# Scores of two head halves side by side on two row halves of TensorE, with product parts and loads put in a new order, in a gated cross-attention and feed-forward layer

## What is computed

```python
x = x + tanh(g_xattn[0]) * attention(layernorm(x), ctx, ctx, Wq, Wk, Wv, Wfc, bfc)
x = x + tanh(g_ffn[0]) * ffn(layernorm(x), router_weight, sh_*, r_*)

# attention: 32 heads of 16, 8 groups of keys and values (4 heads share one)
qh = (q @ Wq.T).reshape(N, S, HEADS, HEAD_DIM).transpose(0, 2, 1, 3)
kh = (k @ Wk.T).reshape(N, S, GROUPS, HEAD_DIM).transpose(0, 2, 1, 3)   # vh alike
score = jnp.einsum('bhqd,bhkd->bhqk', qh, kh) / math.sqrt(HEAD_DIM)
out = jnp.einsum('bhqk,bhkd->bhqd', jax.nn.softmax(score, axis=-1), vh)
return out.transpose(0, 2, 1, 3).reshape(N, S, EMBED) @ Wfc.T + bfc
```

## Time and profile before

| | before |
|---|---|
| median of three runs | 955.55 us (951.3 to 956.73) |
| the profiled execution | 942.72 us |
| its span, first to last instruction | 940.9 us |
| TensorE matmuls busy | 899.5 us (96%) |
| VectorE busy | 646.6 us (69%) |
| GpSimd busy | 486.7 us (52%) |
| ScalarE busy | 343.4 us (37%) |
| mean granted TensorE clock | 0.987 |

### The profile page before, as it was taken

One profiled execution on the slowest core, in us unless ns is written; L12 is line 12 of the kernel. 1 busy time (PEld: TensorE's weight loads), 2 busy tenths in 40 slices (PEclk: granted clock), 3 DMA queues, 4 the chain that ended last, 5 costly groups with the idle time before them and its releaser, 6 DMA issues.

```text
span 940.9 us, 14873 instructions
## 1 busy us (share of the span) xinstructions
PE 899.5 (96%) x4896; PEld 697.8 (74%) x4896; DVE 646.6 (69%) x1083; ACT 343.4 (37%) x637; POOL 486.7 (52%) x485
## 2 busy tenths in 40 slices
PE   4689999999999999999999999999999999999998
PEld 3556766676677665688888888887688888888887
DVE  6678888778878887566656566567766656566566
ACT  5165566556655686212212122136212211122112
POOL 4201201300130299878766696663778766696650
PEclk9789999999999999999999999999999999999999
DMA  8863344435343420211111121111312111121102
GB/s 277 201 144 80 78 116 74 108 80 118 62 96 83 87 37 25 90 45 67 45 60 52 45 67 45 45 57 56 112 45 68 45 54 57 45 67 45 45 1 89
DMA packets 42346, 70.83 MB, mean 75 GB/s; under 512 B 5312, under 2 KB 21184, under 8 KB 42048
## 3 DMA queue, kind: packets, MB, share of 16 engines
q1 hardware_dynamic: 42304, 70.29, 27.9%
HBM read 55.33 MB, written 14.68 MB: 74 GB/s over the span
## 4 chain that ended last, share of the span: by engine, by line
PE 72%; issue 17%; DVE 4%; DMA 3%; POOL 2%; ACT 2%; SPq 0%; POOLq 0%; DVEq 0%; ACTq 0%
PE bank L1241 21%; PE bank L1243 20%; PE bank L1242 20%; PE bank L1316 3%; PE bank L1296 3%; PE bank L1306 3%; PE bank L1246 1%; POOL xa L461 1%; DMA q_scr<-qx_l 1%; POOL cx_l L430 1%; DVE mcol L887 1%; PE bank L1565 1%; DVE x_l L1206 1%; DMA wfc_raw<-wfc 1%; DMA xa<-x 1%
## 5 line engine op out<-in xcount | busy, mean ns | idle before, releaser
L887 DVE TENSOR_REDUCE mcol<-bank 128x2 f32<-128x512 f32 x256 | 169.8, 677 | 48.9 <-PE bank L1296 48.1
L1241 PE MATMUL bank<-x_l,w_h 128*128 128x512 f32 x504 | 197.5, 392 | 2.7 <-DVE u L1077 2.5
L1243 PE MATMUL bank<-x_h,w_h 128*128 128x512 f32 x504 | 196.4, 390 | 0.0
L1242 PE MATMUL bank<-x_h,w_l 128*128 128x512 f32 x504 | 196.4, 390 | 0.0
L740 ACT ACTIVATE probs<-bank 128x512 f32<-128x512 f32 x256 | 150.1, 594 | 120.6 <-PE bank L1306 119.5
L595 ACT ACTIVATE hT_h<-bank 128x512 fp32r<-128x512 f32 x72 | 43.2, 599 | 360.3 <-DVE bank L1179 351.5
L551 POOL TENSOR_TENSOR w_l<-raw,w_h 128x512 fp32r<-128x512 f32 (+1 forms) x144 | 162.1, 1159 | 2.9
L1089 DVE SCALAR_TENSOR_TENSOR xa<-bank,tgf,xa 128x512 f32<-128x512 f32 x128 | 96.1, 751 | 77.7 <-PE bank L1243 77.6
L1296 PE MATMUL bank<-k_st,q_st 65*128 65x256 f32 x512 | 114.0, 312 | 11.8 <-DMA q_st<-q_scr 7.1
L1296 PEld LDWEIGHTS bank<-k_st,q_st 65*128 65x128 f32 x512 | 92.9, 201 | 43.1 <-DVE mcol L887 16.6
L430 POOL TENSOR_TENSOR cx_l<-cx_raw,cx_h 128x512 fp32r<-128x512 f32 x12 | 15.5, 1295 | 191.4 <-ACT cx_h L595 191.4
(11 more groups left out here) (148 smaller groups left out, 1362.8 us busy)
## 6 DMA issues: line engine op xcount, KB each, us to landing
raw<-w_gu SPq DMA_DIRECT2D x36, 512.0 KB, 3.3
q_st<-q_scr SPq DMA_DIRECT2D x96, 128.0 KB, 3.8
dnraw<-w_dn SPq DMA_DIRECT2D x36, 256.0 KB, 2.6
xa<-x SPq DMA_DIRECT2D x4, 1024.0 KB, 7.6
cx_raw<-ctxT SPq DMA_DIRECT2D x16, 256.0 KB, 3.4
q_scr<-qx_h SPq DMA_DIRECT2D x16, 256.0 KB, 2.1
q_scr<-qx_l SPq DMA_DIRECT2D x16, 256.0 KB, 2.2
out<-xa SPq DMA_DIRECT2D x16, 256.0 KB, 2.0
```

What stands on the lines that cost most here:

```text
L887: v.tensor_reduce(mcol[:, par, at:at + 2], bank[u % sm_banks(n)][:, :].rearrange("p (r k) -> p r k", r=2), AX.X, ALU.max).then_inc(max_ok, 1)
L1241: mm(out, a_h, b_l, start=start, stop=False, skip_group_check=onto)
L1242: mm(out, a_l, b_h, start=False, stop=False, skip_group_check=onto)
L1243: return mm(out, a_h, b_h, start=False, stop=stop, skip_group_check=onto)
```

## The change

Heads of a chunk are dealt to two halves of the array's rows: four heads at rows 0 to 63, four at rows 64 to 127. q is stored with half the columns (`QUADS`), its weights are put in another order on the host, and k is read twice, once for each row half. The zero rows and their memset go: `SM` is 48, `MROW` 48, `ST` 49. Units on TensorE become four pairs `v` a step. A pair starts when both maxima (or both exponentials) of the last pair are done. Each half has a bank and semaphores of its own. `read_q` and `read_k` issue six transfers in place of three. `put_max` writes one row in each half.

Parts of products stand behind every pair, up to three at a time, and also cross from one step to the next. Transposes of x use one bank, output parts the other. `aT` has two copies. In SyncE's list writes of q go ahead of the reads, context loads and the write of k ahead of `put_max`. The wait ahead of `read_q` is now for the values' products of step n - 1. `m_copy` follows the fourth exponential instead of the third. `w_h0` and `w_l0` have memory of their own.

```diff
-CONSTS = 2
-SM = P // 2 + 1
+CONSTS = 1
+SM = 3 * DH
 MROW = SM
 ST = MROW + 1
+ROWS = P // 2
+QUADS = HC // 2
...
-        q_st = sb("q_st", [P, CHUNKS, HC, S], f32r, att)
+        q_st = sb("q_st", [P, CHUNKS, QUADS, S], f32r, att)
...
-        aT = sb("aT", [P, S], f32, att)
+        aT = sb("aT", [P, 2, S], f32, att)
...
+            return bank[j] if isinstance(tb, int) and tb == 0 else PJ[0]
+
+        def q_bank(tb, oc):
+
+            return PJ[(oc + 1) % 2] if isinstance(tb, int) and tb == 0 else PJ[1 if oc == 0 else 0]
+
+        def f_bank(t, bb, qt):
+
+            return PJ[qt] if isinstance(t, int) and t == BLOCKS - 1 and bb == 1 else PJ[1]
...
+            def scored(n):
+
+                sp.wait_ge(pv_ok, 4 * n)
...
                 if not fresh:
-                    sp.wait_ge(st_full, UNITS * n)
+                    scored(n)
                 sp.wait_ge(q_wr[c], 32 * (tb + 1))
-                for row, part in ((0, 0), (DH, 0), (2 * DH, 1)):
-                    src = q_scr[part, tb, c, :, bb * S:(bb + 1) * S].rearrange("(h d) q -> d h q", d=DH)
-                    sp.dma_start(r(q_st[row:row + DH, c, :, :]), src).then_inc(q_rd[c], 16)
+                for e in range(2):
+                    for row, part in ((0, 0), (DH, 0), (2 * DH, 1)):
+                        src = q_scr[part, tb, c, e * ROWS:(e + 1) * ROWS,
+                                    bb * S:(bb + 1) * S].rearrange("(h d) q -> d h q", d=DH)
+                        at = e * ROWS + row
+                        sp.dma_start(r(q_st[at:at + DH, c, :, :]), src).then_inc(q_rd[c], 16)
...
+                for e in range(2):
+                    for row, part in ((0, 0), (DH, 1), (2 * DH, 0)):
+                        src = k_scr[part, tb, :, bb * S:(bb + 1) * S].rearrange("(g d) s -> d g s", d=DH)
+                        at = e * ROWS + row
+                        sp.dma_start(r(k_st[at:at + DH, bb, :, :]), src).then_inc(k_rd[bb], 16)
...
                 for s in range(STEPS):
                     n = STEPS * t + s
-                    if s + 3 < STEPS or not last and s != 6:
+                    if s == 0 and not first:
+                        write_q_high(t, 3)
+                        write_q_low(t, 3)
+                    if not last and s >= 5:
+                        write_q_high(t + 1, s - 5)
+                        write_q_low(t + 1, s - 5)
+                    if s + 3 < STEPS or not last:
                         e = s + 3
                         tb = t if e < STEPS else t + 1
                         read_q(tb, e % STEPS // CHUNKS, e % CHUNKS, n, first and s == 0)
...
+                    if s in (0, 2) and not last:
+                        load_cx(t + 1, s)
+                        load_cx(t + 1, s + 1)
+                    if s == 4 and not last:
+                        write_k(t + 1)
                     if not last or s + 1 < STEPS:
                         put_max(n + 1, (s + 1) % CHUNKS)
...
-            g.memset(q_st[0:SM, :, :, :].bitcast(f32), 0.0).then_inc(consts, 1)
...
-                        if u == 2 and (not last or s + 1 < STEPS):
+                        if u == 3 and (not last or s + 1 < STEPS):
                             m_copy(n + 1)
...
+            def sm_pair(n, v, bb, c):
+
+                qt, g2 = v % 2, v // 2
                 banks = sm_banks(n)
-                if not (isinstance(n, int) and n == 0 and u < banks):
-                    pe.wait_ge(max_ok, UNITS * n + u + 1 - banks)
+                if not (isinstance(n, int) and n == 0 and 2 * v < banks):
+                    pe.wait_ge(max_ok, UNITS * n + 2 * v + 2 - banks)
                 for j in range(2):
...
+                    for e in range(2):
+                        rows = slice(e * ROWS, e * ROWS + SM)
+                        last = mm(bank[(2 * v + e) % banks][:, j * S:(j + 1) * S],
+                                  q_st[rows, c, 2 * g2 + j, qt * P:(qt + 1) * P],
+                                  k_st[rows, bb, 2 * c + g2, :], start=True, stop=True)
+                        if j == 1:
+                            last.then_inc(sm_full[e], 1)
+
+            def st_pair(n, v, bb, c):
+
+                kt, g2 = v % 2, v // 2
+                if not (isinstance(n, int) and n == 0 and v == 0):
+                    pe.wait_ge(exp_ok, UNITS * n + 2 * v)
+                for e in range(2):
+                    rows = slice(e * ROWS, e * ROWS + ST)
+                    mm(STB[e][:, :], k_st[rows, bb, 2 * c + g2, kt * P:(kt + 1) * P],
+                       q_st[rows, c, 2 * g2:2 * g2 + 2, :], start=True, stop=True).then_inc(st_full[e], 1)
```

In the last block the output parts of its first tile stand in steps 4 and 5, of its second in step 6, of the last batch in step 7. VectorE's list in the new order:

```diff
+                        if not last and s == 1 and u == 0:
+                            x_low(nx, 1)
+                        if not last and s == 2 and u == 0:
+                            x_low(nx, 3)
+                        if s == 7 and u == 0:
+                            a_low(n - 3, 0, last)
+                        if s == 7 and u == 2:
+                            a_low(n - 2, 1, last)
...
+                        if s == 1 and u == 3 and not first:
+                            f_sum(t - 1, 1, 0)
+                        if s == 2 and u == 1 and not first:
+                            f_sum(t - 1, 1, 1)
...
+                        if s == 6 and u == 1:
+                            f_sum(t, 0, 0)
+                        if s == 7 and u == 1:
+                            f_sum(t, 0, 1)
...
+                        if s == 4 and u == 1:
                             k_low(nx)
-                        if s in (6, 7) and u == 5:
+                        if s == 4 and u == 7:
+                            q_low(nx, 0)
+                        if s == 5 and u == 5:
+                            q_low(nx, 1)
+                        if s in (6, 7) and u == 7:
                             q_low(nx, s - 4)
```

433 lines of the change are left out of this document (213 added, 220 removed).

## The result

The changed kernel is slightly slower. Its median is 961.01 us (952.57 to 963.86, 15 runs) against 952.3 us for the kernel before on the same chip (945.75 to 961.83, 15 runs). The ratio is 1.0083, with a 95% interval of 1.0054 to 1.0112. The prediction was 932.5 us with a range of 911 to 957: wrong in sign, and the time lies outside the range. The profiled execution took 956.5 us with a span of 954.7, where before it took 942.72 and 940.9.

What follows compares the result with a forecast made beforehand. TensorE was taken to bound the middle attention blocks, VectorE less than a fifth behind. Savings of 17.7, 8 and 2 us less 4.7 lost at the start gave 23 us off 955.55, so 932.5 us, range 911 to 957.

Steps and rivals of the forecast that it cites:

- part 5: Loads: running blocks have queue room; before the first step, extra reads of q and k lose 4.7 us, bounds 2 and 8.
- The other moves: Context loads ahead of the maxima's row, x_job in one bank, second aT: free, within 1 us a block either way.
- part 2: Shape changes around each pair on TensorE: 0.19 us for entry and exit, 6.1 us a block; bounds 0 and 0.5 a pair.
- part 1: Score products of both head halves run at once on TensorE: 15.1 us less a block, bounds 0 and 15.1.
- third rival: Row halves run one after the other on TensorE, so pairs save nothing: 15 us slower, 970 us; chance 0.13.
- part 3: Pairs instead of units in the middle blocks: 77 us a block against 86.6 and 85.1, 17.7 us saved.
- the floor of 1.85: Least time of a slot, a pair and what stands behind it: scores, two maxima, release and second half's start, 1.85 us.
- part 4: First and last attention blocks: 8 us saved of 85.9 in the first, 2 us of 70.3 in the last.
- The second: Rival: the row of maxima becomes the last wait, middle blocks 81 us, last 76, kernel 953, no difference; chance 0.13.
- The first: Rival: VectorE and ScalarE hide more than granted, middle blocks 70 to 72 us, 41 us off, 914; chance 0.22.
- halves together: Sign of being right: in a middle block, a pair's two maximum products start within 0.1 us of one another.
- a gap of over 0.3 us without a semaphore: Sign of being wrong: such a gap between a product part and a pair would show the price of shape changes.

Runs made afterwards that it cites:

- the run with fillers: Changed kernel with k read for the first half only, plus unread matmuls at step 2 of every block but the first and three last-block slots: 937.85 us.

## Why the prediction was wrong

**The DMA engines (part 5) are the step that decided the sign.** It said that "In a running block the queue has room", and counted only what the reads of q cost the queue, 2.7 us of 9; the six reads of k are not in that sum. Never counted was how long the 16 engines need: 768 KB of k at some 125 GB/s is 6 us, and the reads of q follow them. The write of q's first chunk, moved behind k's reads and just ahead of its use, is not named there; it falls under "The other moves", which went down as "free, within 1 us a block either way". Against the run with k read once, k's second three reads cost 3.2 us in the third block, 5.9 in the second, and 18.6 up to the attention's end, with the clock's falls behind the waits in it. Over the three traces of that code the two blocks' costs are 3.2 to 5.6 and 2.0 to 5.9. k's doubled bytes do stand in part 5, but only for the start. Bytes and lost slack act together: with k read once the same order costs the third block's step 5 nothing (9.63 us), moving k's reads behind the write didn't help, and with the same bytes one step earlier half or more of the third block's loss went.

**The changes of shape (part 2) were mis-sized by half.** I read the 0.085 ahead of a values block and the 0.105 behind it in rows 4 as an entry and an exit. They are the ends of two changes, each of which costs both: 0.19 us a change, 0.38 a pair, 12.2 us a block instead of 6.1. The bounds (0 to 0.5) held the value; the one taken was wrong. The Trainium skill's "TensorEngine Tiling (Array Packing)", section Tiling Modes, says that a change of mode drains the engine; the trace agrees that a change costs time, 0.19 us of it, and doesn't show what happens in it.

**The overlap (part 1) was right.** The products of both halves start within 0.34 and 0.32 us, changes of shape included, so that a pair takes what one unit took, 15 us less a block as worked out. So the third rival (row halves one after another) is refuted, though the kernel did get slower. The third block's TensorE sum becomes 71.3 + 6.1 = 77.4; the run with k read once shows 75.81 busy.

**The middle blocks (part 3)**: forecast 77, measured 89.34 and 84.77. Of the 20.1 us too many, 11.4 go when k is read once and the clock stays at 1.00 (7.03 and 4.42, against the run with fillers). How they divide between the reads and the clock differs by block: 5.87 and 3.17 go with k read once alone, but in the third block that run has a fall of the clock at step 2 which the changed kernel's trace doesn't have. 8.7 are left for both blocks. The shape changes are 12.2 more in both together than in the sum, and slots at the floor of 1.85 hide part of that; I can't part the rest from what VectorE adds. That VectorE stays under TensorE as a whole but binds in single slots was right, and dearer than thought: in the two middle blocks TensorE waits 8.4 us for maxima where it waited 2.7 before, and a maximum that is 0.26 us shorter gave a block some 3 us.

**First and last block (part 4)**: 8 and 2 us of saving were forecast. From step 1 on, the first block took 77.48 us (66.40 to 143.88) against 74.18 (63.41 to 137.59), and 71.18 in the run with k read once: the reads again. The last block rose by 5.2 us (75.49 against 70.3). There k read once gives 1.6 back, and the filled gaps of steps 2 to 4 another 2.0, which step 6 then took again. 2.4 lie in steps 6 and 7 (17.17 against 14.74 us); the three are more than 5.2, as other steps got shorter. In 6 and 7 I knew of the parts moved in, but let them hide behind the exponentials, which they did not.

**The start (part 5)** was forecast at 4.7 us lost; 3.0 were (66.40 against 63.41), but profiles of the same code there lie 4 us apart, so that the size isn't confirmed.

**The clock** is in no part. The forecast took it as it was, 0.96 to 1.00 in the four blocks of rows 2; after, it was 0.92, 0.94, 0.98 and 0.91. A faster TensorE waits more between slots, and the clock fell behind some of these waits.

**The rivals.** The second (row of maxima last) has the right size of result, 953, for another reason; its wait shows in the third block only as 0.17 us at 293.80 and, once k was read earlier, in step 4. So that 953 lies nearer to the measured time than 932.5 is chance. The first was out of reach with these changes of shape.

**Of the signs named**, halves together came true, and so did the first exponential some 3.5 us later (55.16 against 51.74 us), though profiles of the same code there differ by as much. A pair took 0.66 us instead of 0.5 to 0.6, a middle block not 77. What I named for part 2, a gap of over 0.3 us without a semaphore, did not come, since the price is spread over four places of 0.1. No sign was named for a late read of q.

## What to carry to other kernels

Where a change doubles small-packet transfers, divide their bytes by the rate that such transfers show in the trace, and lay the result beside the step's length; the issue time on the queue is not their cost. For each write that is read back, compare the time between write, read and use before and after, and treat every move that shortens it as a new wait. Read the price of a change of state on both sides of both changes, against the steady spacing of the same instructions. Before a block's length in one trace is compared with another's, look how far traces of the same code lie apart.

## What the runs showed of the hardware

- Two row halves of 48 or 49 rows run side by side: 4 x 256 columns in 0.34 us, 2 x 512 in 0.32, with part of a change of shape in each figure.
- A change to row halves and back costs 0.38 to 0.39 us a pair beyond the products: 0.09 us ahead of the first product of a new shape and 0.105 us behind it. Ahead of and behind a block on column strips stand the same two figures (0.32 and 0.34 instead of 0.235, rows 4).
- Reads of k kept the DMA engines over 90% busy at 113 to 159 GB/s, where writes of q had 380; a write of 256 KB issued behind them took 5.89 us to land instead of 2.2.
- TensorE's granted clock fell from 2.4 to 1.2 GHz during or behind waits of 1.24 to 4.49 us in these steps, and not behind every such wait: behind 1.61 us it stayed at 1.00 in the changed kernel's third block and fell to 0.50 in the run with k read once. With products in the wait at step 2 it stayed at 1.00 in six of six blocks.
